# Copying the first group's middle products out on VectorE, early normalising on VectorE, tanh gates, and new orders, in a two-layer attention, state-space and feed-forward kernel

## What is computed

```python
xn = _layernorm(x)
x = x + _L0_attn_ref(xn, ...) + _L0_ffn_ref(xn, ...)     # layer 0
xn = _layernorm(x)
x = x + _L1_attn_ref(xn, ...) + _L1_ffn_ref(xn, ...)     # layer 1

# layer 0, attention: 16 query heads of 8, 4 key heads; softmax over 256 keys, per sequence
# layer 0, ffn: top-2 gate over 8 experts that share weights: relu(xn @ w1) @ w2, times the gate
# layer 1, "attention": a state-space scan over 256 tokens, 256 channels, 16 states
xs, z = split(xn @ W_in); xs = silu(conv4(xs) + conv_b)
dt = softplus(xs @ W_dt + b_dt); Bs = xs @ W_x
h = h * exp(-A * dt_t) + Bs_t;  y_t = sum(h) + D * xs_t      # one step per token
out = (y * silu(z)) @ W_out
# layer 1, ffn: four ternary layers of width 512
h = silu(tlin(x, w1)) * tlin(x, w2)
h = gelu(tlin(h, h1)); h = gelu(tlin(h, h2)); out = tlin(h, w3)
```

## Time and profile before

| what | us |
|---|---|
| median of three runs | 362.25 |
| the profiled execution | 362.47 |
| its span, first to last instruction | 360.7 |
| TensorE busy | 349.0 |
| VectorE busy | 303.1 |
| ScalarE busy | 299.8 |
| GpSimd busy | 233.1 |

### The profile page before, as it was taken

How to read it: one execution, slowest core, us unless ns; L and a number is a source line. 1 busy time by engine, 2 the same in 40 slices (tenths; PEclk the granted TensorE clock), 3 DMA queues, 4 the chain that set the end, 5 groups by cost and what they waited for, 6 DMA issues and landing times.

```text
span 360.7 us, 5747 instructions
## 1 busy us (share of the span) xinstructions
PE 349.0 (97%) x1754; PEld 180.4 (50%) x1754; DVE 303.1 (84%) x516; ACT 299.8 (83%) x521; POOL 233.1 (65%) x296
## 2 busy tenths in 40 slices
PE   7999999999999999998999999999999999999996
PEld 4566544747565423433244447444455644464546
DVE  5889889978898885498899788999999999888950
ACT  4966876778679977999998889989999999589660
POOL 3266625314411602226999687999999999988990
PEclk9999999999999999999999999999999999999999
DMA  6268496571645303000000000000001000000000
GB/s 223 83 158 153 96 251 170 90 131 35 109 104 70 120 1 121 23 0 2 0 0 0 25 0 22 2 15 2 0 2 36 0 30 1 2 0 1 16 15 29
DMA packets 28942, 19.26 MB, mean 53 GB/s; under 512 B 4240, under 2 KB 27888, under 8 KB 28656
## 3 DMA queue, kind: packets, MB, share of 16 engines
q1 hardware_dynamic: 28912, 18.90, 22.5%
HBM read 13.32 MB, written 5.37 MB: 52 GB/s over the span
## 4 chain that ended last, share of the span: by engine, by line
PE 77%; ACT 12%; DVE 4%; issue 3%; POOL 2%; DMA 1%; ACTq 0%; DVEq 0%; POOLq 0%
PE bank L1028 13%; PE bank L1016 11%; PE bank L436 7%; PE bank L423 4%; PE bank L400 4%; PE bank L1099 4%; ACT da L1207 4%; PE bank L460 4%; PE bank L468 4%; PE bank L1005 4%; PE bank L1006 4%; PE bank L989 3%; PE bank L1052 3%; PE bank L1072 3%; ACT pt L631 3%
## 5 line engine op out<-in xcount | busy, mean ns | idle before, releaser
L1340 POOL TENSOR_TENSOR acc<-acc,hb 128x512 f32<-128x512 f32 x128 | 158.4, 1269 | 20.8 <-DVE hb L1284 20.6
L1284 DVE TENSOR_TENSOR_SCAN hb<-da,bank 128x512 f32<-128x512 f32 x128 | 146.3, 1201 | 13.9 <-PE bank L989 12.4
L681 DVE TENSOR_REDUCE mx<-bank 128x2 f32<-128x512 f32 x128 | 81.4, 680 | 9.9 <-PE bank L400 7.7
L1207 ACT ACTIVATE da<-dt,nega 128x510 f32<-128x510 f32 x128 | 81.7, 713 | 0.2
L1028 PE MATMUL bank<-gelu,ld 128*128 128x512 f32 x128 | 58.5, 593 | 1.1 <-ACT gelu L1195 1.0
L1016 PE MATMUL bank<-sil,ld 128*128 128x512 f32 x128 | 59.2, 592 | 0.0
L631 ACT ACTIVATE pt<-bank 128x512 f32<-128x512 f32 x72 | 39.7, 603 | 4.3 <-PE bank L423 2.7
L423 PE MATMUL bank<-q_st,k_st 51*128 51x512 bf16 (+1 forms) x128 | 39.0, 381 | 2.8 <-ACT pt L631 2.5
L1028 PEld LDWEIGHTS bank<-gelu,ld 128*128 128x128 f32 x128 | 24.0, 190 | 28.2 <-issue 27.2
L400 PE MATMUL bank<-k_st,q_st 48*128 48x256 bf16 x240 | 37.0, 272 | 0.4 <-DVE mx L681 0.2
L1016 PEld LDWEIGHTS bank<-sil,ld 128*128 128x128 f32 x128 | 23.6, 190 | 22.8 <-issue 22.0
(11 more groups left out here) (161 smaller groups left out, 540.5 us busy)
## 6 DMA issues: line engine op xcount, KB each, us to landing
q_st<-q_scr SPq DMA_DIRECT2D x15, 192.0 KB, 5.4
q_st<-q_scr SPq DMA_DIRECT2D x7, 384.0 KB, 5.0
ld<-in_pack SPq DMA_DIRECT2D x2, 1024.0 KB, 5.0
q_scr<-qk_parts SPq DMA_DIRECT2D x8, 192.0 KB, 3.9
k_st<-k_scr SPq DMA_DIRECT2D x14, 96.0 KB, 4.9
q_scr<-qk_parts SPq DMA_DIRECT2D x8, 128.0 KB, 2.6
out<-x SPq DMA_DIRECT2D x8, 128.0 KB, 1.9
ld<-in_pack SPq DMA_DIRECT2D x1, 968.0 KB, 7.5
```

Source lines behind the costliest of these rows:

```text
L681: eng.tensor_reduce(mx[:, 2 * pair:2 * pair + 2, q], score_bank(b, n)[:, :].rearrange("p (h k) -> p h k", h=2), AX.X, ALU.max).then_inc(mx ...
L1207: act(da(n)[:, :, 1:T], dt[:, g % 2, c, :].rearrange("p (b n) -> p b n", b=GB)[:, :, 1:T], ACT.Exp, scale=nega[:, c, s:s + 1]).then_inc(da ...
L1284: eng.tensor_tensor_scan(hb[:, s % NPAIR, c, :], da(n).rearrange("p b n -> p (b n)"), b_bank(g, s)[:, :], 0.0, ALU.mult, ALU.add).then_inc ...
L1340: TT(acc[:, g % 2, c, :], acc[:, g % 2, c, :], hb[:, s % NPAIR, c, :], ALU.add).then_inc(add_ok, 1)
```

## The change

It has these parts:

1. **Lifts.** For blocks 0 and 1 of group 0, VectorE copies the middle product out of its bank: `lift2` into `xc` (ahead of `gelu` 0 and 1), `lift3` into `gelu3` (ahead of `hid` 0 and 1, in place). TensorE waits for the copy, where it waited for the gelu, before it writes blocks 2 and 3. In the ScalarE order the four gelus of group 0 now stand together, and so do the last four of each kind in group 3.
2. **Early normalising.** `normalise` of groups 0 and 1 leaves ScalarE (four activations each); VectorE does it as `early_normalise` (four `tensor_scalar` each). GpSimd's `shifted` of the first half goes.
3. **Tanh gates.** `TANH_X` is (0, 1) in place of (0,): the x gates of group 1 are tanh on ScalarE and two more `xm` on VectorE.
4. **Waits.** `gelu_last` and `gated` no longer wait for the last batch's residual (`x1_ok`), but for its last product with the values (`pv_ok`) and for the transposes of it (`ot_ps`). `taps` of group 2 gets a wait for the first two gelus, which now read `xc`.
5. **Orders.** All five strings are new.

The diff without the orders:

```diff
@@ -227,7 +226,7 @@
             "negm_ok", "msplit", "h_ps", "h_ok", "v_ps", "v_ok", "srt_ok", "gex_ok", "gch",
             "f_ps", "y_ok", "s_ps", "mx_ok", "st_ps", "p_ok", "pv_ok", "o_ok", "ot_ps", "rd_ok",
             "on_ok", "oT_ps", "oT_ok", "w_ps", "x1_ok", "gr_ok")]
-    done.update(xn_ok=xn_ok, xb_ok=xb_ok, v_ok=v_ok, srt_ok=srt_ok, stk_ok=stk_ok, p_ok=p_ok, on_ok=on_ok, o_ok=o_ok, x1_ok=x1_ok, st_ps=st_ps, pv_ok=pv_ok, mx_ok=mx_ok, y_ok=y_ok)
+    done.update(xn_ok=xn_ok, xb_ok=xb_ok, v_ok=v_ok, srt_ok=srt_ok, stk_ok=stk_ok, p_ok=p_ok, on_ok=on_ok, o_ok=o_ok, x1_ok=x1_ok, ot_ps=ot_ps, st_ps=st_ps, pv_ok=pv_ok, mx_ok=mx_ok, y_ok=y_ok)
     NRUN = len(Q_RUNS)
     NMR = NPART
     NGC = 8
@@ -857,7 +856,7 @@
 NPAIR = 4
 ND0, ND1, ND2 = 6, 17, 8
 NRD = ND0 + ND1 + ND2
-TANH_Z, TANH_X, TANH_FFN = (0, 1, 2, 3), (0,), (0,)
+TANH_Z, TANH_X, TANH_FFN = (0, 1, 2, 3), (0, 1), (0,)
 
 
 def early_buffers(sb):
@@ -919,16 +918,17 @@
 
     (i_act, nm_ok, zm_ok, xm_ok, t1_ok, da_zero, st_ok, sd_ok, rs_ok, i_pool, xn_ok, xT_ps, xT_ok, l1_ps, sil_ok, h0_ok, win_ps, z_ok, cv_ok, conv,
      xs_ok, dt_ps, dt_ok, bx_ps, bx_ok, bsp, b_put, b_got, b_ps, da_ok, scan, acc_in, add_ok, y_ok, l2_ps, g2_ok,
-     l3_ps, g3_ok, oy_ps, o_ps, o_ok, out_ok) = [sem("b_" + n) for n in (
+     l3_ps, g3_ok, oy_ps, o_ps, o_ok, out_ok, lift2_ok, lift3_ok) = [sem("b_" + n) for n in (
          "i_act", "nm_ok", "zm_ok", "xm_ok", "t1_ok", "da_zero", "st_ok", "sd_ok", "rs_ok", "i_pool", "xn_ok", "xT_ps", "xT_ok", "l1_ps", "sil_ok", "h0_ok",
          "win_ps", "z_ok", "cv_ok", "conv", "xs_ok", "dt_ps", "dt_ok", "bx_ps", "bx_ok", "bsp", "b_put", "b_got",
          "b_ps", "da_ok", "scan", "acc_in", "add_ok", "y_ok", "l2_ps", "g2_ok", "l3_ps", "g3_ok", "oy_ps", "o_ps",
-         "o_ok", "out_ok")]
+         "o_ok", "out_ok", "lift2_ok", "lift3_ok")]
     NXB = 3
     NIA = 6
     NBS = 3
     NPI = 4
     PARTS = ((0, 2 * GTT), (2 * GTT, NT))
+    EARLY_G = 2
 
     def z_done(eng, g, k):
 
@@ -1011,7 +1011,7 @@
                 reached(eng, h0_ok, g, KC, KC)
                 if g == 0:
                     eng.wait_ge(done["ld"][2], 16)
-                    reached(eng, g2_ok, g, KC, c - 1)
+                    reached(eng, lift2_ok, g, 2, c - 1)
             for k in range(2 * half, 2 * half + 2):
                 last = mm(f_bank(g, c)[:, :], h1[:, k, c * P:(c + 1) * P], sil[:, k, :],
                           start=(k == 0), stop=(k == KC - 1))
@@ -1023,7 +1023,7 @@
                 reached(eng, g2_ok, g, KC, KC)
                 if g == 0:
                     eng.wait_ge(done["ld"][3], 16)
-                    reached(eng, g3_ok, g, KC, c - 1)
+                    reached(eng, lift3_ok, g, 2, c - 1)
             for k in range(2 * half, 2 * half + 2):
                 last = mm(f_bank(g, c)[:, :], h2[:, k, c * P:(c + 1) * P], g2[:, k, :],
                           start=(k == 0), stop=(k == KC - 1))
@@ -1131,6 +1131,8 @@
             reached(eng, win_ps, g, 4, c + 1)
             if g > 0:
                 x_done(eng, g - 1)
+            if g == 2:
+                reached(eng, g2_ok, 0, KC, 2)
             act(xc[:, c, :], (pA, pB)[c][:, :], ACT.Identity, bias=t["cb"][:, c:c + 1],
                 scale=t["cw"][:, c, TAPS - 1:TAPS]).then_inc(cv_ok, 1)
 
@@ -1153,9 +1155,9 @@
             last.then_inc(xs_ok, 1)
 
         def normalise(g):
-            part = 0 if g < PARTS[0][1] // GTT else 1
             reached(eng, xT_ps, g - 2, 1, 1)
-            eng.wait_ge(nm_ok, 2 * part + 2)
+            eng.wait_ge(xn_ok, EARLY_G)
+            eng.wait_ge(nm_ok, 2)
             for q in range(GTT):
                 c = g * GTT + q
                 last = act(xn[:, g % 2, q, :], x1[:, c, :], ACT.Identity, bias=nmean[:, c:c + 1], scale=rstd[:, c:c + 1])
@@ -1180,19 +1182,27 @@
                 scale=0.5 if g in TANH_X else 1.0).then_inc(dt_ok, 1)
 
         def gelu_mid(g, c):
-            reached(eng, l2_ps, g, 2 * KC, 2 * c + 2)
+            lifted = g == 0 and c < 2
+            if lifted:
+                reached(eng, lift2_ok, g, 2, c + 1)
+            else:
+                reached(eng, l2_ps, g, 2 * KC, 2 * c + 2)
             reached(eng, l3_ps, g - 1, 2 * KC, 2 * KC)
             if g == 0:
                 settled(eng, done["mx_ok"], NB * NH)
                 settled(eng, done["st_ps"], NB * NH)
-            act(g2[:, c, :], f_bank(g, c)[:, :], ACT.Gelu, scale=t["h1s"][:, c:c + 1]).then_inc(g2_ok, 1)
+            act(g2[:, c, :], xc[:, c, :] if lifted else f_bank(g, c)[:, :], ACT.Gelu, scale=t["h1s"][:, c:c + 1]).then_inc(g2_ok, 1)
 
         def gelu_last(g, c):
-            reached(eng, l3_ps, g, 2 * KC, 2 * c + 2)
+            lifted = g == 0 and c < 2
+            if lifted:
+                reached(eng, lift3_ok, g, 2, c + 1)
+            else:
+                reached(eng, l3_ps, g, 2 * KC, 2 * c + 2)
             reached(eng, o_ps, g - 1, 2, 2)
             if g == 0:
-                settled(eng, done["x1_ok"], NB)
-            act(g3[:, c, :], f_bank(g, c)[:, :], ACT.Gelu, scale=t["h2s"][:, c:c + 1]).then_inc(g3_ok, 1)
+                settled(eng, done["pv_ok"], 4 * NB)
+            act(g3[:, c, :], g3[:, c, :] if lifted else f_bank(g, c)[:, :], ACT.Gelu, scale=t["h2s"][:, c:c + 1]).then_inc(g3_ok, 1)
 
         def decay(n):
             g, s, c = n // (2 * NS), n // CI % NS, n % CI
@@ -1223,7 +1233,7 @@
             last.then_inc(i_act, 1)
 
         return dict(
-            deviation=deviation, normalise=normalise, decay_rates=decay_rates, x_out=x_out, b_in=b_in,
+            deviation=deviation, normalise=lambda n: normalise(EARLY_G + n), decay_rates=decay_rates, x_out=x_out, b_in=b_in,
             sil=lambda n: ffn_silu(n // KC, n % KC),
             gelu=lambda n: gelu_mid(n // KC, n % KC), hid=lambda n: gelu_last(n // KC, n % KC),
             taps=lambda n: taps(n // CI, n % CI), gate_x=lambda n: gate_x(n // CI, n % CI),
@@ -1251,6 +1261,16 @@
             reached(eng, xs_ok, g, 2, c + 1)
             STT(xs[:, g % 2, c, :], xs[:, g % 2, c, :], 1.0, xc[:, c, :], ALU.add, ALU.mult).then_inc(xm_ok, 1)
 
+        def lift2(c):
+            reached(eng, l2_ps, 0, 2 * KC, 2 * c + 2)
+            x_done(eng, 1)
+            eng.tensor_copy(xc[:, c, :], f_bank(0, c)[:, :]).then_inc(lift2_ok, 1)
+
+        def lift3(c):
+            reached(eng, l3_ps, 0, 2 * KC, 2 * c + 2)
+            settled(eng, done["pv_ok"], 4 * NB)
+            eng.tensor_copy(g3[:, c, :], f_bank(0, c)[:, :]).then_inc(lift3_ok, 1)
+
         def other_taps(g, c):
             acc_v = xc[:, c, :].rearrange("p (b n) -> p b n", b=GB)
             src_v = (pA, pB)[c][:, :].rearrange("p (b n) -> p b n", b=GB)
@@ -1272,6 +1292,14 @@
             lo, hi = PARTS[part]
             eng.wait_ge(sd_ok, part + 1)
             eng.reciprocal(rstd[:, lo:hi], std[:, lo:hi]).then_inc(rs_ok, 1)
+
+        def early_normalise(g):
+            eng.wait_ge(rs_ok, 1)
+            for q in range(GTT):
+                c = g * GTT + q
+                last = eng.tensor_scalar(xn[:, g % 2, q, :], x1[:, c, :], mv[:, c, 0:1], rstd[:, c:c + 1],
+                                         ALU.subtract, ALU.mult)
+            last.then_inc(xn_ok, 1)
 
         def scans(g, s):
             reached(eng, b_ps, g, NS, s + 1)
@@ -1308,7 +1336,7 @@
                 eng.memset(da_2[:, :, :, 0:1], 0.0).then_inc(da_zero, 1)
 
         return dict(
-            statistics=statistics, inverse1=inverse, clear=clear, residual1=lambda n: residual(n // 2, n % 2),
+            statistics=statistics, inverse1=inverse, lift2=lift2, lift3=lift3, early_normalise=early_normalise, clear=clear, residual1=lambda n: residual(n // 2, n % 2),
             mul=lambda n: ffn_mul(n // KC, n % KC), zm=lambda n: z_mul(n // CI, n % CI),
             xm=lambda n: x_mul(n // CI, n % CI), conv=lambda n: other_taps(n // CI, n % CI),
             scan=lambda n: scans(n // NS, n % NS))
@@ -1321,7 +1349,7 @@
             lo, hi = PARTS[part]
             eng.wait_ge(rs_ok, part + 1)
             TT(nmean[:, lo:hi], mv[:, lo:hi, 0], rstd[:, lo:hi], ALU.mult).then_inc(nm_ok, 1)
-            eng.wait_ge(nm_ok, 2 * part + 1)
+            eng.wait_ge(nm_ok, 1)
             eng.tensor_scalar(nmean[:, lo:hi], nmean[:, lo:hi], -1.0, None, ALU.mult).then_inc(nm_ok, 1)
 
         def start_acc(g, c):
@@ -1344,7 +1372,7 @@
             z_done(eng, g, c + 1)
             reached(eng, oy_ps, g - 1, 1, 1)
             if g == 0:
-                settled(eng, done["x1_ok"], NB)
+                settled(eng, done["ot_ps"], NB)
             TT(y[:, c, :], acc[:, g % 2, c, :], zs[:, g % 2, c, :], ALU.mult).then_inc(y_ok, 1)
 
         def split(g):
@@ -1368,7 +1396,7 @@
                               t["w3s_bc"][:, :].rearrange("p (o n) -> p o n", o=1).broadcast_to([P, KC, P]),
                               ALU.mult).then_inc(i_pool, 1)
 
```

(2 more changed lines are left out.)

105 lines of the change are left out of this document (52 added, 53 removed).

## The result

The changed kernel is a little faster. Over 20 runs of each, the median is 362.31 us (358.33 to 367.15) against 363.43 us for the kernel before (362.14 to 366.82); the ratio is 0.9933, 95% interval 0.9908 to 0.9958. That ratio leaves out the three slowest runs of the changed kernel (363.86, 364.44 and 367.15 us), as runs in a slower state; the medians of all runs have a ratio of 0.9969. Measured once more with the first series of experiments (`after_again`), it took 359.94 us against 362.85 us, ratio 0.9916 (0.9883 to 0.9949). The profiled execution took 359.47 us, span 357.7 us; the sum of the prediction was 360.1 us against the profiled time and 359.8 us against the median.

What follows compares the result with a forecast made beforehand. TensorE, busy 349.0 of 360.7 us, bounds most of the kernel; VectorE was taken to decide the handover. Terms -2.5 - 0.5 + 0.4 + 0.9 - 1.2 + 0.5 = -2.4 us gave 360.1 us profiled, 359.8 us median (356.8 to 363.3).

Steps and rivals of the forecast that it cites:

- Handover: From layer 0 to layer 1, first scan to group 2's convolution: 2.5 us gained (0 to 3.5).
- the bound of 3.5 us: In the handover: with 56.8 us of work VectorE could finish at most 3.5 us sooner.
- So VectorE decides this stretch: First scan to group 2's convolution: VectorE's 3.5 us limit is below ScalarE's 4.6 and TensorE's 4.3 us idle.
- ScalarE decides, and the lifts are hidden: Rival for the handover: lifts fill VectorE's waits, all of ScalarE's 4.6 us is gained; about 357 us, chance 0.17.
- Table loads: ScalarE: 32 loads for 43; five fewer in the handover save 6.4 us, the six elsewhere save nothing.
- Early normalising: Layer 0 to 1, 105 to 146.5 us: normalising moved to VectorE gives -0.5 us, between -0.7 and +2.7.
- Both are covered by TensorE, which has 0.7 us to give: Early normalising: VectorE's added 2.7 us and ScalarE's eight removed activations hide behind TensorE, so at most 0.7 us.
- The order of layer 0: New TensorE order: +0.4 us for fewer shared pairs, +0.9 us for array changes, -1.2 us for saved waits.
- the start: Four more dummy matmuls ahead of the first transposes cost +0.5 us; the later-issued third part of x costs 0.
- the terms of A, S and the array changes: TensorE in layer 0: 97 A-S pairs for 99, +0.4 us; 144 whole/partial array changes for 135, +0.9 us.
- The 0.1 us per change: TensorE in layer 0: each change between whole and partial array use, up to 0.19 us, taken at half size.
- The gain doesn't arrive: Rival: GpSimd's tail or layer 0's costs at their upper ends eat the gain; 361.8 us, chance 0.26.

Runs made afterwards that it cites:

- lift2_scalar: The changed kernel with the two copies of the second product on ScalarE instead of VectorE; 359.63 us, ratio 0.9913 to the kernel before.
- late_lifts_narrow: loads_late with the four lifts copying 64 of 512 columns, part of the products left out; 358.07 us, ratio 0.9827 to the kernel before.
- lifts_double: The changed kernel with each of the four lifts done twice; 362.59 us, ratio 0.9967 to the kernel before.
- late_lift3_scalar: loads_late with the two copies of the third product on ScalarE instead of VectorE; 358.46 us, ratio 0.9838 to the kernel before.
- late_tanh_off: loads_late with silu back on the second group's x gates: two more table loads, two fewer VectorE operations; 362.28 us, ratio 0.9955 to the kernel before.
- late_tanh_order: late_tanh_off with one product (1.72 us of matmuls) moved up in TensorE's order into its wait; 360.6 us, ratio 0.9891 to the kernel before.
- before_tanh: The kernel before with only the second group's x gates as tanh and two more VectorE operations; 364.68 us, ratio 1.0042 to the kernel before.
- late_tail_split: loads_late with ScalarE's last gelus and decays split much as before, six more table loads; 358.05 us, ratio 0.9864 to the kernel before.
- late_early_off: loads_late with normalising of the first two groups back on ScalarE and its shift on GpSimd; 360.93 us, ratio 0.9924 to the kernel before.
- loads_late: The changed kernel with the third weight load (1 MB) moved later in SyncE's order, behind batch 6's last rows; 357.67 us, ratio 0.9849 to the kernel before.
- E16: Not a run: an exp instruction, by its start time a mark in the trace; 48.20 us before, 47.64 us after, 47.54 us in loads_late.
- before_load_early: The kernel before with the third weight load moved ahead of the sixth batch's keys; 364.36 us, ratio 1.0007.

## Why the prediction was right, and where it was not

The sum against the profiled time was -2.4 us; the profiled executions differ by 3.0 us. The ratio 0.9933, taken of 362.25 us, is -2.4 us to the tenth. That is luck: several terms missed by more than the 0.6 us that separate sum and profile, and they cancelled. Term by term:

**Handover, -2.5 us forecast: -3.3 us measured** (60.36 to 57.07 us), under the bound of 3.5 us. There are 32 table loads, no lift waits for more than 0.18 us, the lifts take 667 and 686 ns (0.68 forecast), and `x_transposes2` is 1.9 us ahead. The first lift and the last, from VectorE in order of time after:

```profile
167.91 0.67 DVE L1267 COPY xc<-bank 128x512 f32<-128x512 f32 x1
...
195.47 0.69 DVE L1272 COPY gelu<-bank 128x512 f32<-128x512 f32 x1 [0.18 <-PE bank L1028]
```

But the step "So VectorE decides this stretch" failed. It was a coincidence of sizes: VectorE had room for 3.5 us, TensorE had 4.0 us of idle time to give. With 1.1 us (`lift2_scalar`) or 1.9 us (`late_lifts_narrow`) of VectorE's work taken away, nothing moved. TensorE's own matmuls are the floor, and the change brought the stretch to 0.9 us above it. VectorE, full at 55.62 of 57.07 us, is the next bound, 1 us behind (`lifts_double`), and ScalarE's way to the root the third (`late_lift3_scalar`). What the lifts themselves gain was not measured: the runs show that they cost nothing, but none leaves them out, and none has the new orders without them. How the 3.3 us divide between lifts, gates and orders stays open.

**The rival "ScalarE decides, and the lifts are hidden"** was right in its second half: the lifts are hidden. It did not give its 4.6 us, since TensorE ran out first.

**Table loads.** Of the five in the handover, the two that the tanh gates save were measured. They are worth 3.9 to 4.6 us in the new order (`late_tanh_off`), their own 2.6 us in the stretch once TensorE's order is fitted to them (`late_tanh_order`), and less than nothing in the old order (`before_tanh`). The last group's six are worth nothing (`late_tail_split`). The same 1.28 us has several prices, by what stands behind the load.

The Trainium skill ("ScalarE: Activation LUTs", What ACT_TABLE_LOAD costs) adds a drain of about the load's own length. ScalarE in order of time after shows none:

```profile
185.62 1.24 ACT L1194 ACTIVATE gelu<-bank,ld 128x512 f32<-128x512 f32 x2
186.88 1.28 ACT L1181 ACT_TABLE_LOAD   x1
188.17 1.26 ACT L1181 ACTIVATE dt<-bank,ld 128x512 f32<-128x512 f32 x2
```

The load starts 0.02 us behind the last gelu and the softplus 0.01 us behind the load. Here a switch costs 1.3 us and not 2.66.

**Early normalising, -0.5 us forecast, at most -0.7: worth 2.7 to 3.3 us** (`late_early_off`). The failed step is "Both are covered by TensorE, which has 0.7 us to give". I read TensorE's idle time in the kernel before as the most that could be won. But the copies' price belongs to the new order, in which `o_out` stands right behind them; an order that leaves them out can be packed closer. The prices of parts in a packed order don't add up to its gain: this one and the tanh gates' make 6.6 us or more, and `loads_late` is 4.65 us ahead of the kernel before in the profiles. The operation itself takes 412 ns for the 343 that I took.

**The order of layer 0, +0.4 +0.9 -1.2, and the start, +0.5 us.** With early normalising that is +0.1 us up to the first scan. `loads_late` has -1.20 us there, the changed kernel +0.45, with the load's 1.66 us in it. The first exp was 1.06 us late, twice the forecast for the dummy matmuls, and by `E16` this was more than regained. No run measures the terms of A, S and the array changes one by one. The 0.1 us per change, taken as half of one difference, can be read in the trace of before: from the start of a line 468 piece to the next instruction it is 1.79 us with no A or S on either side, 1.88 to 1.89 with one on one side, and 1.98 with one on both.

**What was missed** is the SyncE order behind the start. The prediction looked at the third part of `x`, and did not follow the weight loads through the new string: 1.66 us in the profile, and about 3 us more (363.0 for 359.7 us) in the twelve of twenty runs whose clock fell, as far as it is this wait that they fell behind. It explains why the median moved by 1.1 us where the profiled run moved by 3.0: `loads_late`, without it, takes 357.67 us, 2.3 us less than `after_again` on the same chip. The load alone is not the whole reason, since in the old order it cost nothing that can be told (`before_load_early`). "The gain doesn't arrive", at 361.8 us, is the rival that the median came nearest to, but not for its reasons: GpSimd's `y` ends at 348.30 us, 1.07 us ahead of the `out` that needs it, and layer 0's order saved more than it cost.

## What to carry to other kernels

Two engines can have the same slack; to learn which one decides, take work away from each in turn as well as adding some: doubling a cost shows only who is next. A price found by taking one part out of a packed order holds for that order and place. Follow every transfer through a new order of the DMA queue, the big ones that nobody waits for above all, and look at what small one stands behind them. And judge a loss that only some runs have by the clock of the single runs: one profile shows a kernel with or without it, the median mixes both.

## What was not expected of the hardware

- A wait of TensorE of 1.97, 2.16 or 2.88 us was followed by 3 to 7 us at a granted clock of 0.50; waits of 1.17 and 1.62 us were not. In `late_early_off` a wait of 1.34 us with one of 0.22 us close behind was followed by it too. And in the profiles of `before_tanh` and `before_load_early` the clock fell at 39 and at 42 us, for some 3 and 7 us, with no wait of TensorE over 0.31 us in the 10 us before. So the length of one wait alone doesn't tell, and not every lost clock comes of a wait.
- One 1 MB load ahead of it made a 96 KB transfer take 8.56 us from issue to landing, where `loads_late` has 3.8 to 6.2 us for the same kind at the same place.
- 128x512 float32 copied out of a bank takes 0.67 to 0.69 us on VectorE; 128x64 takes 0.20 to 0.23 us: a third of the time for an eighth of the columns.
